# Cross-attention and a 32-expert layer in one kernel: the probabilities of a token step are split and turned first, and each expert's third transposes move between two products

## The reference

```python
x = x + attention(layernorm(x), ctx)        # 8 heads of 64, 64 context rows in each batch
y = layernorm(x)
s = sigmoid(y @ gate_w.T)                   # 32 experts, the 4 best by s + bias, weights s / sum(s)
h = silu(xe @ W1[e]) * (xe @ W3[e])         # xe: up to 512 rows of each expert e
out = x + sum(weight * (h @ W2[e])) + silu(y @ sw1.T) * (y @ sw3.T) @ sw2.T
```

## Time and profile before

| | |
|---|---|
| median of 3 runs | 1758.38 us |
| the profiled execution | 1757.34 us |
| its span, first to last instruction | 1755.5 us |
| mean granted TensorE clock | 0.982 of full |
| busy share of the span | PE 94%, DVE 77%, ACT 65%, POOL 64% |

### The profile page before, as it was taken

The page is one execution under the profiler, slowest core; times in us unless marked ns, Lnnn a source line. Parts: engine busy times, 40 slices in busy tenths (PEclk is TensorE's granted clock), DMA queues, the critical chain, the costliest instruction groups (busy, mean ns, idle before and its releaser), DMA issues.

```text
span 1755.5 us, 32521 instructions
## 1 busy us (share of the span) xinstructions
PE 1643.0 (94%) x9061; PEld 1021.2 (58%) x9061; DVE 1359.3 (77%) x3651; ACT 1148.2 (65%) x2496; POOL 1124.1 (64%) x978
## 2 busy tenths in 40 slices
PE   5999999999999999999999999999977999999997
PEld 4555566556655656565666656555534555555554
DVE  4678787878888788888888788888875777777775
ACT  4777777777777777777777777777643444444442
POOL 1327777767777777777777777777766454444455
PEclk8999999999999999999999999999998999999999
DMA  8758977765665566655656656666646876688852
GB/s 298 192 133 231 220 174 168 168 156 128 136 146 138 129 135 150 146 143 128 141 137 132 133 130 145 138 144 165 134 94 191 222 197 162 163 200 198 200 140 25
DMA packets 466888, 277.01 MB, mean 158 GB/s; under 512 B 341839, under 2 KB 384079, under 8 KB 466708
## 3 DMA queue, kind: packets, MB, share of 16 engines
q1 hardware_dynamic: 407316, 244.99, 54.7%
q0 software_dynamic: 59392, 29.94, 10.7%
HBM read 135.06 MB, written 223.08 MB: 204 GB/s over the span
## 4 chain that ended last, share of the span: by engine, by line
PE 34%; DVE 24%; ACT 17%; issue 15%; DMA 5%; SPq 3%; ACTq 1%; DVEq 0%; POOL 0%; POOLq 0%
PE GE_ps L1572 6%; PE UE_ps L1572 6%; PE O_ps L484 5%; PE YE_ps L1610 4%; PE S_ps L469 3%; ACT done L841 3%; DVE top_s L1297 3%; DMA pt_l<-p_l 3%; PE G_ps L511 2%; DVE x_l L1238 2%; DVE S_ps L1303 2%; ACT xt_h L751 2%; SPq L394 2%; ACT xr L851 2%; ACT waste L704 2%
## 5 line engine op out<-in xcount | busy, mean ns | idle before, releaser
L929 POOL DMA_INDIRECT slot_rows<-xr,slot x480 | 517.2, 1078 | 132.6 <-issue 125.8
L1559 POOL DMA_INDIRECT out<-ye,token x128 | 198.9, 1554 | 207.5 <-DMA out<-ye,token 90.3
L939 POOL TENSOR_TENSOR xt_l<-xt,xt_h 128x512 fp32r<-128x512 f32 x128 | 163.9, 1281 | 204.4 <-ACT xt_h L751 204.2
L792 ACT ACTIVATE prob<-S_ps,rs 128x512 f32<-128x512 f32 x128 | 88.1, 688 | 248.7 <-DVE S_ps L1303 248.7
L484 PE MATMUL O_ps<-m_h,pt_h 128*128 128x512 f16 x512 | 197.9, 386 | 43.1 <-DMA pt_l<-p_l 41.9
L469 PE MATMUL S_ps<-a_h,xt_h 128*128 128x512 f32 x512 | 212.1, 414 | 2.4 <-DVE m_l L1276 2.4
L469 PE MATMUL S_ps<-a_h,xt_l 128*128 128x512 f32 x512 | 201.3, 393 | 0.0
L469 PE MATMUL S_ps<-a_l,xt_h 128*128 128x512 f32 x512 | 201.0, 393 | 0.0
L484 PE MATMUL O_ps<-m_h,pt_l 128*128 128x512 f16 x512 | 196.5, 384 | 0.0
L484 PE MATMUL O_ps<-m_l,pt_h 128*128 128x512 f16 x512 | 196.3, 383 | 0.0
L954 POOL TENSOR_TENSOR prob<-prob,rsum 128x512 f32<-128x512 f32 x128 | 134.9, 1054 | 70.0 <-DVE rsum L1331 68.1
(11 more groups left out here) (257 smaller groups left out, 4636.1 us busy)
## 6 DMA issues: line engine op xcount, KB each, us to landing
rows<-slot_rows SPq DMA_DIRECT2D x128, 280.0 KB, 3.4
xt<-in_xT SPq DMA_DIRECT2D x128, 256.0 KB
xr<-in_x SPq DMA_DIRECT2D x64, 512.0 KB, 4.0
out<-done SPq DMA_DIRECT2D x64, 512.0 KB, 3.2
up_more<-in_w SPq DMA_DIRECT2D x36, 256.0 KB, 4.4
slot_rows<-xr SPq DMA_DIRECT2D x16, 560.0 KB, 5.6
slot_rows<-xr,slot POOLq DMA_INDIRECT x512, 3.2
up_w<-in_w SPq DMA_DIRECT2D x28, 256.0 KB, 4.6
```

The source lines that it names most:

```text
L792: act.activation(prob[:, t % 2, :, :], S_ps[t % 2][:, :].rearrange("p (h j) -> p h j", h=H), ACT.Exp, scale=rs[:, q % 2, 0, t % 2:t % 2 + ...
L929: pool.indirect_dma_start(slot_rows, bass.IndirectOffsetOnAxis(ap=slot[:, g % 2, i, q:q + 1], axis=0), xr[:, t % (4 * XRING), :], None, bo ...
L939: pool.tensor_tensor(xt_l[:, t % 2, :, :], xt[:, t % 2, :, :], xt_h[:, t % 2, :, :].bitcast(F32), ALU.subtract).then_inc(xt_lo, 1)
L1559: pool.indirect_dma_start(out, bass.IndirectOffsetOnAxis(ap=token[:, e % RING, c:c + 1], axis=0), ye[:, e % 4, c, :], None, bounds_check=T ...
```

## The change

In the token loop `p_h` becomes ACT's first instruction of each step, ahead of `xt_h`. `p_l` moves on DVE from behind the subtraction of the maxima to a place ahead of `a_l` or `m_l`. On SP the transposes of the probabilities come ahead of those of the normalised rows in every step; before, they did so in the last two steps alone. Special cases of the last step go away with this.

In the experts, PE turns chunk 2 between the `GE_ps` and the `UE_ps` products of the second half. ACT's `tanh(u, 1)` then stands ahead of `turned_hi(t, 2)`, and DVE's `gate(u, 1)` ahead of `turned_lo(t, 2)`.

```diff
 # SP, step(n)
                     t = at(n, MIX)
-                    if t is not None and t >= FINAL - 1:
+                    if t is not None:
                         turn_probabilities(t)
                     t = at(n, X2)
                     if t is not None:
                         turn_rows(t)
...
-                    t = at(n, MIX)
-                    if t is not None and t < FINAL - 1:
-                        turn_probabilities(t)
 # ACT, step(n)
+                    t = at(n, MIX)
+                    if t is not None:
+                        act.wait_ge(prob_done, t + 1)
+                        after(act, p_turned, t * 32)
+                        act.activation(p_h[:, :], prob[:, t % 2, :, :].rearrange("p h j -> p (h j)"), ACT.Copy,
+                                       scale=P_SCALE).then_inc(p_hi, 1)
                     t = at(n, XT_SPLIT)
...
                     t = at(n, X2)
                     if t is not None:
-                        rows_scaled(t)
-                        if n < TAIL - 1:
-                            rows_high(t)
+                        normal_rows(t)
...
-                    t = at(n, MIX)
-                    if t is not None:
-                        act.wait_ge(prob_done, t + 1)
-                        after(act, p_turned, t * 32)
-                        act.activation(p_h[:, :], prob[:, t % 2, :, :].rearrange("p h j -> p (h j)"), ACT.Copy,
-                                       scale=P_SCALE).then_inc(p_hi, 1)
-                    if n == TAIL - 1:
-                        rows_high(FINAL - 4)
 # DVE, step(n)
                     roots(n, 0)
+                    if s9 is not None:
+                        low_probabilities(s9)
                     b, j = chunk_at(n, 2)
...
                     roots(n, 3)
                     if weights is not None:
                         weigh_ops(weights, 2)
-                    if s9 is not None and n < TAIL - 1:
-                        low_probabilities(s9)
 # experts, PE
             up_half(GE_ps[c], e, 0, c).then_inc(ge_done, 1)
+            if between is not None:
+                turn(between, 2)
             if e:
                 pe.wait_ge(hie_done, (e - 1) * 2 + c + 1)
             up_half(UE_ps[c], e, I, c).then_inc(ue_done, 1)
...
                 turn(t, 1)
+            if u is not None:
+                up(u, 1, t)
+            elif t is not None:
                 turn(t, 2)
-            if u is not None:
-                up(u, 1)
```

More of the change, by code:

```diff
@@ L1285, in step @@
                         slot_list(slots)
-                    if s13 is not None and n < TAIL - 1:
-                        rows_low(s13)
-                    if n == TAIL - 1:
-                        low_probabilities(s9)
+                    if s13 is not None:
                         rows_low(s13)
@@ L1575, in up_half, with up @@
             return last
-        def up(e, c):
+        def up(e, c, between=None):
             if c == 0:
@@ L1672, in step @@
                 turned_hi(t, 1)
+            if u is not None:
+                tanh(u, 1)
+            if t is not None:
                 turned_hi(t, 2)
             if u is not None:
-                tanh(u, 1)
                 widen_down(u)
@@ L1743, in step @@
                 turned_lo(t, 1)
+            if u is not None:
+                gate(u, 1)
+            if t is not None:
                 turned_lo(t, 2)
             if u is not None:
-                gate(u, 1)
                 hidden(u, 1)
```

## The result

The changed kernel takes 1808.82 us (median of 4 runs, 1807.28 to 1810.95), the kernel before 1760.35 in the same comparison: ratio 1.0273, 95% interval 1.0237 to 1.0310, so 2.7% slower. The profiled execution took 1810.95 us with a span of 1809.1, 53.6 us above the span of 1755.5 before. In the changed kernel the lines are numbered anew; the names are the same.

What follows compares the result with a forecast made beforehand. The prediction took waits among ACT, DVE and POOL to pace the token loop, with PE following. Token loop +79, returned waits -14 and experts -24 gave +41 us: 1799 us, eight-in-ten range 1764 to 1826.

Steps and rivals of the forecast that it cites:

- a ring over ACT, DVE and POOL: Token loop: these engines waiting on one another set the step pace; PE, busy 94% of the span, only follows.
- the round: Token loop: four successive steps, 38.76 us before, forecast 2.80 us longer; over 28.25 rounds +79 us.
- `p_h`, 0.53 in kinds 0 and 1: First two steps of each four in the token loop: `p_h` ahead of `xt_h` delays ACT, +0.53 us each.
- Kind 2, 1.08: Third step of each four: `p_l` on DVE keeps out POOL's `xt_l`, so `ht_l` and `x_l` come later, +1.08 us.
- kind 3, 0.66: Fourth step of each four: 0.53 us from `p_h` plus 0.13 as POOL's `xt_l` waits for DVE's `p_l`.
- What returns, 14: Token loop: of PE's 41.9 us of waits, 14 us return, through ACT's 17.1 us of waits for `hid`.
- The start and the end of the loop, nothing: Token-loop steps ahead of step 18 and behind step 131: no net cost.
- The experts, 24: Experts: ending PE's waits for `xe_l` before chunk 2's transposes saves 24 us; ends 0 and 27.
- The marks: Forecast trace signs: longer steps, `O_ps` free of `pt_l`, PE waiting for POOL, `x_l` behind `ht_l`, experts 0.72 us closer.
- `p_h` waits for POOL's product: Rival, token loop: `p_h` at ACT's head waits for POOL's product, delaying everything behind it; 1827 us, 13%.
- PE as the bound: Rival, whole kernel: PE sets the pace, so ending its waits saves 66 us; 1692 us, 8%.
- the ring absorbs part: Rival, token loop: third step of four hides `p_h` and `p_l`, POOL never waits for DVE; 1765 us, 9%.

## Why the prediction was right, and where its sizes were off

The forecast was 1799 us, within 1764 to 1826, and the way was the one it gave: a ring over ACT, DVE and POOL sets the token loop's pace, and the change ends two waits of PE while making that ring longer. The run with less work for PE and the run with a shorter ring show the first, the two halves apart show that the loss is the token loop's. That the sum came within 10 us of the measured time is luck in part: as shown below, the round was priced too high and the other terms too low.

*`p_h`, 0.53 in kinds 0 and 1.* Measured 0.52 and 0.51. Its old place became idle time, as told.

*Kind 2, 1.08; kind 3, 0.66.* Measured 0.87 and 0.47. The mechanism in kind 2 was right and its size 0.21 too large: `p_l` ran when it was forecast, but `xt_l`, begun 0.06 us later, was lengthened by 0.46 instead of waiting for the whole `p_l`, and `x_l` started at +4.20, not +4.40. In kind 3 the push of 0.13 did not occur. The round came out at +2.37, not +2.80: 67 us over 28.25 rounds instead of 79. The Trainium skill (SBUF — State Buffer, Who interferes with whom) says that the operation that started first keeps the other out; the trace now shows both sides: `xt_l` 1.75 behind `p_l`, `member` 1.34 behind `ht_l`. It shows them not quite whole: `p_l` still ran for 0.63 us when `xt_l` began, and `xt_l` was 0.46 longer for it.

*What returns, 14.* 67.0 - 57.3 = 9.7, what is left of the round's price over the whole loop. It came back where it was forecast: in the changed kernel no `hid` of the loop waits for PE any more, 17.1 us before.

*The start and the end of the loop, nothing.* +4.1 and +4.7. This price was wrong in sense too: the steps ahead of 18 and behind 131 have `p_h` at their head as well. That their ACT is in the same ring is the likely reason; it was not tried apart.

*The experts, 24.* The term that was mis-sized most. The turns came closer by 0.81 us per expert, 25.3 in all, but the time from the first turn to the end fell from 428.6 to 416.2, by 12.4. The prediction asked whether chunk 3 would be late next; it did not ask what follows the last product. Before, POOL's chain of scatters caught up in the last experts and began the last four 1.2 us after the last `ye`; at PE's new pace it begins them 14 us after it. The run with fewer loads shows that the loads beside the scatters lengthen the chain's pitch, by enough to hold the end. By the reference's routing of these inputs experts 1, 2, 5, 10, 14, 16, 17, 19 to 21, 23, 24 and 28 have more than 512 tokens each and the others 128 at most. In both traces just the scatters behind these start 14 to 17 us after the ones before; the others follow after 9 to 13 us, except behind expert 0. That full rows are the reason was not tried.

Sum: +67.0 - 9.7 + 8.7 - 12.4 = +53.6, which is the difference of the spans. The round was priced 12 us too high, the return, the ends and the experts together 25 too low: +41 against +53.6. The first error hid half of the others.

*The marks.* `O_ps` does not wait for `pt_l`; PE waits at the down products, 37.3 us that the trace puts down to "issue" (by the program it waits for `ht_l` there, and in the trace each of these waits of more than 0.3 us in the loop ends 0.1 us behind an `ht_l`); it does not wait for `xt_l` before the scores, which was forecast too. `x_l` of kind 2 stands right behind `ht_l`. `p_h` waits for POOL's product only 4.1 us in ten steps.

*The rivals.* PE as the bound falls by the result, in which its waits are gone and the time is longer, and by the run with less work for it. That the ring absorbs part falls: each kind shows at least 0.47. That `p_h` waits for POOL's product falls by the 4.1 us.

## What to carry to other kernels

Before ending a wait of a busy engine, look for who is late because of it: PE stood 42 us here and little of that came back (10 us), while 0.5 us at the head of ACT's step went into the time in every step. The gain lay in the ring: taking one operation that the maxima did not need out of it brought 34 us, and only behind that, with PE as the bound, did a late turn of the probabilities cost 46. Find the ring first. A queue that is worked off in order is part of it: reordering two turns made ACT wait for the one that had come first before. Price a gain up to the last instruction of the program: a chain behind the bound engine that just keeps up now takes over at the new pace.

## What was not expected of the hardware

- Less work for PE made the program slower: 80 us less of busy time, +13 us. Behind an idle 4.73 us its granted clock was 0.53 to 0.61 for 8 us, and ACT, which needed its products in that step, waited for them.
- A scatter of 128 rows that adds into HBM landed 7.8 us (median) after its issue beside the loads of rows and weights, 6.3 with fewer weights loaded, in experts 20 to 24; in experts 26 and 27 of the changed kernel, which have 0 and 3 tokens by the reference's routing, 2.9.
- Of two SBUF operations of DVE and POOL that meet, the later one was shown as longer, not as starting later, and by a little less than the overlap: `xt_l` by 0.46 where `p_l` still ran for 0.63 us, and not at all in kind 3, where `p_l` still ran for 0.13 (it started at 877.78 and took 0.69).
